# The closing normalisations and the W1 slices of an expert layer: which engine does them

## The reference

```python
x = x + _layernorm(_L0_attn_ref(_layernorm(x), ...))
x = x + _layernorm(_L0_ffn_ref(_layernorm(x), ...))
# inside _L0_ffn_ref:
y = _layer_norm(x + _mha(x, Wqkv, bqkv, Wo, bo), g1, be1)
idx = argmax(y @ Wg.T)                        # one of 8 experts for each token
moe = relu(y @ W1[idx] + b1[idx]) @ W2[idx] + b2[idx]
z = _layer_norm(y + moe, g2, be2)             # W1: 8 x 128 x 512, W2: 8 x 512 x 128
```

## Time and profile before

| | us |
|---|---|
| median of 3 runs | 722.99 |
| the runs | 721.63, 722.99, 728.51 |
| the profiled execution, its own time | 718.0 |
| its span, first to last instruction | 715.9 |
| PE, DVE, ACT, POOL busy in the span | 575.5, 428.6, 348.5, 333.9 |
| mean granted clock of TensorE | 0.891 |

### The profile page before, as it was taken

How to read it: one execution, slowest core, us unless ns; L and a number is a source line. 1 busy time by engine, 2 the same in 40 slices (tenths; PEclk the granted TensorE clock), 3 DMA queues, 4 the chain that set the end, 5 groups by cost and what they waited for, 6 DMA issues and landing times. The chain is left out here.

```text
span 715.9 us, 16711 instructions
## 1 busy us (share of the span) xinstructions
PE 575.5 (80%) x5511; PEld 428.5 (60%) x5511; DVE 428.6 (60%) x1212; ACT 348.5 (49%) x927; POOL 333.9 (47%) x579
## 2 busy tenths in 40 slices
PE   4899999999999999999834898888874059999400
PEld 3566666666666666666523787777753059998400
DVE  2454576766666666666313787878974316778630
ACT  1024566556656656655621798878640002343330
POOL 5312123332333322321236247777778601689886
PEclk9558999999999999999975999999996569999855
DMA  5000000000000000000025000000011245677223
GB/s 151 10 2 2 3 3 16 18 17 16 8 12 18 17 17 18 17 16 18 17 45 155 1 1 3 1 1 0 8 36 42 82 127 153 161 180 179 32 26 29
DMA packets 33168, 29.73 MB, mean 42 GB/s; under 512 B 4121, under 2 KB 27457, under 8 KB 33090
## 3 DMA queue, kind: packets, MB, share of 16 engines
q1 hardware_dynamic: 25906, 23.55, 12.7%
q0 software_dynamic: 6640, 4.92, 4.6%
q10 hardware_dynamic: 544, 0.26, 0.1%
HBM read 18.24 MB, written 8.12 MB: 37 GB/s over the span
## 5 line engine op out<-in xcount | busy, mean ns | idle before, releaser
L383 DVE TENSOR_REDUCE nmax<-psA 128x2 f32<-128x512 f32 x256 | 165.1, 688 | 120.7 <-PE psA L206 120.5
L511 ACT ACTIVATE pr<-psB 128x512 f32<-128x512 f32 x250 | 135.8, 595 | 123.8 <-PE psB L223 123.1
L206 PE MATMUL psA<-km,q 24*128 24x256 f32 x768 | 138.9, 425 | 3.8 <-POOL km L603 2.1
L223 PE MATMUL psB<-q,km 26*128 26x256 f32 (+1 forms) x752 | 109.9, 411 | 0.0
L206 PEld LDWEIGHTS psA<-km,q 24*128 24x128 f32 x768 | 91.3, 196 | 29.4 <-issue 17.5
L603 POOL TENSOR_TENSOR km<-kraw,rows_of 128x768 f32<-128x768 f32 x16 | 23.5, 1466 | 118.1 <-DVEq L362 113.9
L237 PE MATMUL psO<-pr,v 128*32 128x256 f32 x1024 | 69.4, 389 | 1.3 <-ACT osb L505 1.1
L223 PEld LDWEIGHTS psB<-q,km 26*128 26x128 f32 (+1 forms) x752 | 69.0, 189 | 0.2 <-issue 0.2
L1587 POOL DMA_INDIRECT out<-wz,ys x39 | 63.1, 1618 | 9.2 <-issue 7.4
L577 POOL TENSOR_SCALAR ve<-mv_r 128x2 f32<-128x2 f32 x16 | 3.7, 231 | 123.6 <-DVE mv_r L344 123.6
L1473 DVE TENSOR_TENSOR hT<-psH,e_nb1T 128x512 f32<-128x512 f32 x39 | 27.0, 692 | 42.5 <-PE psH L1434 31.1
(11 more groups left out here) (202 smaller groups left out, 1214.6 us busy)
## 6 DMA issues: line engine op xcount, KB each, us to landing
own<-W SPq DMA_DIRECT2D x39, 256.0 KB, 2.7
ys<-y_sorted SPq DMA_DIRECT2D x39, 72.0 KB, 2.2
xs<-x_all SPq DMA_DIRECT2D x16, 128.0 KB
out<-x_all SPq DMA_DIRECT2D x16, 128.0 KB, 3.7
e_w<-W SPq DMA_DIRECT2D x4, 512.0 KB
x_all<-x SPq DMA_DIRECT2D x1, 1536.0 KB, 10.1
q<-mT SPq DMA_DIRECT2D x64, 4.0 KB
out<-wz,ys POOLq DMA_INDIRECT x39, 3.4
```

What stands on the lines that cost most here:

```text
L206: last = T.matmul(psA[:, n % 2, c * L1:(c + 1) * L1], queries(b, h, depth, slice(c * P, (c + 1) * P)), keys(b, h, depth, slice(0, L1)), st ...
L223: last = T.matmul(bank_of(b, h)[:, c * L1:(c + 1) * L1], keys(b, h, depth, slice(c * P, (c + 1) * P)), queries(b, h, depth, slice(0, L1)), ...
L383: V.tensor_reduce(nmax[:, b % 2, :, h], psA[:, n % 2, :].rearrange("p (c m) -> p c m", c=2), AX.X, ALU.max, negate=True).then_inc(S["a_fre ...
L511: A.activation(pr[:, h % PRING, :, :].rearrange("p c l -> p (c l)"), bank_of(b, h), ACT.Exp, scale=SCALE1).then_inc(S["b_free"], 1)
```

## The change

In its core:

```diff
-            V.tensor_scalar(w1_i[:, :], owner[:, :], float(P), None, ALU.mult).then_inc(S["owner_ok"], 1)
+            V.tensor_scalar(w1_i[:, :], owner[:, :], float(DF), None, ALU.mult).then_inc(S["owner_ok"], 1)
...
-    t = {"w2": [P, NF, NE * P], "b1n": [NE * NF, P], "b2r": [1, NE * P], "g2r": [P, P],
+    t = {"w1": [P, NE * DF], "w2": [P, NF, NE * P], "b1n": [NE * NF, P], "b2r": [1, NE * P], "g2r": [P, P],
          "be2r": [P, P], "nb1T": [P, NE * NF], "b1T": [P, NE * NF], "b2p": [P, NE * P], "top": [P, P]}
     t = {name: ctx.enter_context(nc.sbuf_tensor("e_" + name, shape, F32)) for name, shape in t.items()}
-    loads = [(t["w2"][:, f, :].rearrange("p (e d) -> p e d", d=P),
+    loads = [(t["w1"][:, :].rearrange("p (e f) -> p e f", f=DF), W1.rearrange("e d f -> d e f"))]
+    loads += [(t["w2"][:, f, :].rearrange("p (e d) -> p e d", d=P),
...
-        own = sb("own", [P, 4, DF])
+        own = sb("own", [P, 3, DF])
...
-                pe.wait_ge(S[f"own{t % 4}"], 16 * (t // 4 + 1))
+                pe.wait_ge(S["own_ok"], t + 1)
...
-                dve.wait_ge(S[f"agg{kind}"], g)
+                dve.wait_ge(S[f"rs{kind}"], g)
                 for k in range(SIZES[g]):
                     last = V.bn_aggr(mv[kind][:, k, :], st[kind][:, k, :])
                 last.then_inc(S[f"mv{kind}"], 1)
-                dve.wait_ge(S[f"mv{kind}"], g + 1)
+
+            def scales(kind, g):
+                n, s = SIZES[g], g % 2
+                dve.wait_ge(S[f"sd{kind}"], g + 1)
                 if g >= 2:
-                    dve.wait_ge(S[f"rs{kind}"], g - 1)
-                n = SIZES[g]
-                V.tensor_scalar(nm[kind][:, g % 2, 0:n], mv[kind][:, 0:n, 0], -1.0, None, ALU.mult)
-                V.tensor_scalar(ve[kind][:, g % 2, 0:n], mv[kind][:, 0:n, 1], EPS, None, ALU.add
-                                ).then_inc(S[f"agg{kind}"], 1)
+                    dve.wait_ge(S["w_ok" if kind else "z1_ok"], ends(g - 2))
+                V.reciprocal(rs[kind][:, s, 0:n], sd[kind][:, 0:n]).then_inc(S[f"inv{kind}"], 1)
+                dve.wait_ge(S[f"inv{kind}"], g + 1)
+                V.scalar_tensor_tensor(out=nb[kind][:, s, 0:n], in0=mv[kind][:, 0:n, 0], scalar=-1.0,
+                                       in1=rs[kind][:, s, 0:n], op0=ALU.mult, op1=ALU.mult
+                                       ).then_inc(S[f"rs{kind}"], 1)
...
+                if (g := at(t, 4)) is not None:
+                    scales(0, g)
+                if (g := at(t, 10)) is not None:
+                    scales(1, g)
...
+            def fetch(t):
+                e = act.value_load(w1_i[0:1, t:t + 1], min_val=0, max_val=(NE - 1) * DF)
+                if t >= 3:
+                    act.wait_ge(S["h_full"], t - 2)
+                A.activation(own[:, t % 3, :], w["w1"][:, bass.ds(e, DF)], ACT.Copy).then_inc(S["own_ok"], 1)
...
+            def deviation(kind, g):
+                n = SIZES[g]
+                act.wait_ge(S["consts"], 1)
+                act.wait_ge(S[f"mv{kind}"], g + 1)
+                act.wait_ge(S[f"inv{kind}"], g)
+                A.activation(sd[kind][:, 0:n], mv[kind][:, 0:n, 1], ACT.Sqrt, bias=eps[:, :]
+                             ).then_inc(S[f"sd{kind}"], 1)
...
+            fetch(0)
             turned(0)
+            fetch(1)
             turned(1)
             for t in range(STEPS):
                 if t + 2 < NS:
+                    fetch(t + 2)
                     turned(t + 2)
...
+                if (g := at(t, 3)) is not None:
+                    deviation(0, g)
+                if (g := at(t, 9)) is not None:
+                    deviation(1, g)
...
-            def scale(kind, g):
-                n, s = SIZES[g], g % 2
-                pool.wait_ge(S[f"agg{kind}"], g + 1)
-                if g >= 2:
-                    pool.wait_ge(S["w_ok" if kind else "z1_ok"], ends(g - 2))
-                G.tensor_tensor(rs[kind][:, s, 0:n], ve[kind][:, s, 0:n], half4[:, 0:n], ALU.pow
-                                ).then_inc(S[f"pow{kind}"], 1)
-                pool.wait_ge(S[f"pow{kind}"], g + 1)
-                G.tensor_tensor(nb[kind][:, s, 0:n], nm[kind][:, s, 0:n], rs[kind][:, s, 0:n], ALU.mult
-                                ).then_inc(S[f"rs{kind}"], 1)
...
-                if (g := at(t, 3)) is not None:
-                    scale(0, g)
-                if (g := at(t, 9)) is not None:
-                    scale(1, g)
...
-            rows = W1.rearrange("e d f -> (e d) f")
-
-            def fetch(t):
-                e = sp.value_load(w1_i[0:1, t:t + 1], min_val=0, max_val=(NE - 1) * P)
-                if t >= 4:
-                    sp.wait_ge(S["h_full"], t - 3)
-                sp.dma_start(own[:, t % 4, :], rows[bass.ds(e, P), :]).then_inc(S[f"own{t % 4}"], 16)
-
-            def load(t):
+            sp.wait_ge(sent, 16 * NT)
+            for t in range(NS):
                 r = sp.value_load(row_i[0:1, t:t + 1], min_val=0, max_val=LAST_ROW - P)
                 if t >= RING:
...
-            for t in range(4):
-                fetch(t)
-            sp.wait_ge(sent, 16 * NT)
-            for t in range(6):
-                load(t)
-            for t in range(NS):
-                if t + 6 < NS:
-                    load(t + 6)
-                if t + 4 < NS:
-                    fetch(t + 4)
```

More of the change, by code:

```diff
@@ L1359, in expert_weights, with experts @@
     return t, loads
-def experts(nc, w, W1, ident, kept, sorting, sent, y_sorted, out):
+def experts(nc, w, ident, kept, sorting, sent, y_sorted, out):
     with ExitStack() as ctx:
@@ L1381, in experts @@
         mv = [sb(f"mv_z{k}", [P, 4, 2]) for k in range(2)]
-        nm = [sb(f"nm_z{k}", [P, 2, 4]) for k in range(2)]
-        ve = [sb(f"ve_z{k}", [P, 2, 4]) for k in range(2)]
+        sd = [sb(f"sd_z{k}", [P, 4]) for k in range(2)]
         rs = [sb(f"rs_z{k}", [P, 2, 4]) for k in range(2)]
         nb = [sb(f"nb_z{k}", [P, 2, 4]) for k in range(2)]
-        half4 = sb("half4", [P, 4])
+        eps = sb("eps", [P, 1])
         psT, psH, psO = pb("psT"), pb("psH"), pb("psO")
-        names = ["consts", "t_full", "yT_ok", "h_full", "h_ok", "o_full", "z0_ok", "st0", "st1", "mv0",
-                 "mv1", "agg0", "agg1", "pow0", "pow1", "rs0", "rs1", "z1_ok", "z2_step", "z2_ok", "w_ok"]
-        names += [f"own{r}" for r in range(4)] + [f"ys{r}" for r in range(RING)] + [f"put{r}" for r in range(WRING)]
+        names = ["consts", "t_full", "yT_ok", "own_ok", "h_full", "h_ok", "o_full", "z0_ok", "st0", "st1", "mv0",
+                 "mv1", "sd0", "sd1", "inv0", "inv1", "rs0", "rs1", "z1_ok", "z2_step", "z2_ok", "w_ok"]
+        names += [f"ys{r}" for r in range(RING)] + [f"put{r}" for r in range(WRING)]
         S = {n: ctx.enter_context(nc.semaphore("ex_" + n)) for n in names}
@@ L1433, in hidden @@
                 for f in range(NF):
-                    last = T.matmul(psH[t % 2][:, f * P:(f + 1) * P], own[:, t % 4, f * P:(f + 1) * P],
+                    last = T.matmul(psH[t % 2][:, f * P:(f + 1) * P], own[:, t % 3, f * P:(f + 1) * P],
                                     yT[:, t % 3, :], start=True, stop=True)
@@ L1570, in _ @@
             G = nc.gpsimd
-            G.memset(half4[:, :], -0.5).then_inc(S["consts"], 1)
-            pool.wait_ge(S["consts"], 1)
-            def scale(kind, g):
-                n, s = SIZES[g], g % 2
-                pool.wait_ge(S[f"agg{kind}"], g + 1)
-                if g >= 2:
-                    pool.wait_ge(S["w_ok" if kind else "z1_ok"], ends(g - 2))
-                G.tensor_tensor(rs[kind][:, s, 0:n], ve[kind][:, s, 0:n], half4[:, 0:n], ALU.pow
-                                ).then_inc(S[f"pow{kind}"], 1)
-                pool.wait_ge(S[f"pow{kind}"], g + 1)
-                G.tensor_tensor(nb[kind][:, s, 0:n], nm[kind][:, s, 0:n], rs[kind][:, s, 0:n], ALU.mult
-                                ).then_inc(S[f"rs{kind}"], 1)
+            G.memset(eps[:, :], EPS).then_inc(S["consts"], 1)
             def put(t):
@@ L1658, in build_program @@
                          minus_half, xs, y_all, logits, w, loaded, loads, y_sorted, slots, slot_i, base, sorting, sent)
-        experts(nc, w, a["W1"], ident, kept, sorting, sent, y_sorted, out)
+        experts(nc, w, ident, kept, sorting, sent, y_sorted, out)
 def kernel(L0_attn_x, L0_attn_w_qkv, L0_attn_b_qkv, L0_attn_w_o, L0_attn_b_o, L0_ffn_Wqkv, L0_ffn_bqkv, L0_ffn_Wo,
```

## The result

The changed kernel took 702.16 us (median; 701.39 to 709.53, 4 runs), beside 725.75 us for the kernel before in the same runs: a ratio of 0.970 (95% interval 0.9625 to 0.9775). Two later measurements of both kernels gave 0.977 (0.9707 to 0.9834) and 0.970 (0.9648 to 0.9757), with medians of 708.33 and 703.22 against 724.0 and 723.6. By the three pairs of medians the saving is 16 to 24 us. The forecast was 706 us, with 16.5 us saved.

The account below looks back on a forecast made before the run. VectorE was taken to bound the stream from tile 11, POOL's put queue the end. Span 715.9 - 3.3 - 13.2 = 699.4, saving 16.5 us; from the 722.99 median that gives 706 us, range 697 to 715.

Parts of the forecast that it names:

- Start: Start of the experts' stage: without W1 fetches the first `ys` load issues 4.9 us earlier, worth 4.6 after a table load.
- The copy: ScalarE's W1 fetch per tile: 0.48 us plus 0.4 register load, hidden with 0.37 us of room per tile.
- Table load: ScalarE's change to Sqrt: one load suffices, charged 0.3 us, bounds 0 and 1.3.
- The rival with loads in pairs: ScalarE: table loads around every square root, 35 us over the forecast, 741 us; chance 0.05.
- Stream: Tiles 11 to 38, paced by VectorE: 9.69 us per four tiles, tile 38's `hT` at 667.6, 3.3 us earlier.
- rival B: VectorE's cycle is shorter, 9.1 us per four tiles: 702 us, or 698 at PE's pace throughout; chance 0.14.
- Tail: Tile 38's `hT` to the last put's end: 28.2 us against 41.4 before, 13.2 saved.
- Rival D: GpSimd's puts do not draw together, still one each 2.6 us at the end: 8 us lost, 714; chance 0.04.
- recorded signs of being wrong: Profile after: VectorE waits for `sd_z`, ScalarE shows no idle time, or table loads come in pairs.
- The median: Whole kernel: the 16.5 us saving taken from the timed runs' median, 722.99, gives 706.5, called 706.

Follow-up runs that it names:

- the deviations alone: Only the deviations moved (square root on ScalarE, reciprocal and product on VectorE), W1's slices by DMA as in the kernel before: 711.06 us, 0.980 of before.

## Why the prediction was right

The direction, the range (697 to 715) and the mechanism held: the powers left GpSimd, its closing queue shrank from 41 us to 28, and VectorE set the pace from tile 11 on. Not all terms were right, and the sum owes something to luck. Point by point.

*Start.* Forecast 4.6 us saved, measured 10.8 to 6.1, 4.7. The assumption that the sends had landed holds. But 0.6 to 1.1 us are given back between tile 0 and tile 11 (23.0 and 23.3 before, 23.9 to 24.1 after), a cost that the forecast had at nothing. With the slices by DMA this part was 23.2. ScalarE's copies do not stand in PE's way there: in the timeline of the start PE waits only for `ys` (0.71 us before the second transposition) and then has no gap. What differs is its clock. It stays at half speed for 6.9 us after the first transposition, 6.7 and 6.8 in the other two profiles of this kernel, against 4.0 and 4.6 in the kernel before and 4.9 with the deviations alone, whose eight products with W2 take 1.06 us at the place where the changed kernel's take 1.61. Why the clock rises later was not tried.

*The copy.* 0.63 us alone, and 0.52 with others behind it, against 0.48 with bounds of 0.48 to 0.60, with 0.35 us for the register load where 0.4 was taken. Free, and by more than forecast, as the doubled copy shows.

*Table load.* One, 1.28 us, in front of the first square root; that one came 0.40 us late for VectorE. The `hT` of the steps around it are 2.09 to 2.15 apart, so it cost nothing where 0.3 was charged. The rival with loads in pairs fell. By the Trainium skill (ScalarE: Activation LUTs, What ACT_TABLE_LOAD costs) a drain should add 1.38 us; here the engine was idle for 1.30 before the load and ran the square root 0.02 after it, so no run shows that cost on the path.

*Stream.* This is the term that was mis-sized. The forecast was 66.3 us from tile 11 to 38, 1.3 more than before; measured were 63.0, 2.0 less. Two of its parts were off. A `scales` was taken at 0.43, a dependent pair at 0.21 each; the rows show 0.29, since only the product waits for the reciprocal, and the next instruction follows the product after 0.08. And the gap in front of `hT` behind the aggregates fell from about 0.57 to 0.43 with the two small instructions between gone, which I had held constant in the middle of the forecast and let fall in rival B. Per four tiles: 2 x 0.29 more, and the two steps with moments 0.41 and 0.45 less, a net of -0.3 where +0.3 was forecast. The sum also mixed two bases: 9.69 is 0.30 over the one cycle of 9.39 in the earlier trace rows, while the mean of six before was 9.51; on the mean the same working gives 58.9 us from tile 11 to 35 and not 58.1, further from the 55.3 measured. The pace is rival B's 9.1 per four tiles, though its gap of 0.32 is not reached.

*Tail.* Forecast 28.2, measured 28.3 to 28.5. Put 28 starts 8.14 us after tile 38's `hT` (forecast 7.6 + 0.55), and the puts draw together, 1.88 apart. Rival D fell. That 8.14 meets the forecast so closely is luck: `wz` of tile 28 is there 7.05 us after that `hT`, 1.1 earlier than the working had it (each of three `scales` is 0.14 cheaper, and the last two aggregates stand behind the scales and not before, among smaller differences). The puts of tiles 26 and 27 are still in front, although the forecast said that POOL is not behind then. The small queue took up what VectorE was early. Of the recorded signs of being wrong, one showed in part: VectorE does wait for `sd_z`, 2.6 us in all, though not in the steady stream. The square root was expected to be late once, by 0.5 (0.41 in the row), and was so five times in the tail; behind the puts' queue this cost nothing that shows.

*The median.* In the stage 19 us were won where 16.5 were forecast. The kernel before had medians of 723.6 to 725.75 in all later measurements, and the profile that I had was 5.6 to 7.8 us below that, of which the pad writes explain 5. I had set the saving against the median and not against that profile (701.5 would have come out), which this confirms: the hold is in both kernels and drops out of the difference. What is left of the distance between 706 and 702 is the stream's 3 us and the spread of the two stages before, whose end (DVE's last index) lies between 561.0 and 569.3 us in the fourteen profiles of this study, with the 2 MB transfer and without it.

## What to carry to other kernels

Follow the wait chain to the engine that closes the kernel, but then size the stream behind it by the distance of starts on its busiest in-order engine: here VectorE, whose register load of 0.3 to 0.4 us in front of each `hT`, movable in a few lines, gave 5.2 us in the stage, more than the whole resident copy of W1 (3.7 to 4.4). An operation that waits for another engine's small result can go on an engine with room as long as its in-order neighbours leave a step in between; the square root had one in the stream, and cost nothing there. A term that comes out to the hundredth can still hide two errors: look at what the instruction itself waited for, not only at when it started. One profile of an execution can be several us from the median for a cause outside the change; when the two disagree, set the saving, not the end, against the median.

## What the runs showed of the hardware that I had not expected

A direct DMA issued while GpSimd issues indirect ones can take its engine far longer than 1.1 us: eight writes took 16.2 to 16.5 us on SyncE (ten profiles), 15.3 on ScalarE, and four took 3.8 us once the sends had landed. It is not an even 2 us a write. In the changed kernel's third profile the eight start at 558.98, 562.4, 566.6 and 570.9 and then 1.0 to 1.1 apart, while the last send is issued at 568.1. The instructions of the pad line, of the changed kernel's second profile and then of the kernel before's first one (durations in ns, min/median/max):

```profile
L1335 SPq MOVE y_sorted<-zeros x8: 13/29/704, 562.1 to 578.0; - x8
```

```profile
L1335 SPq MOVE y_sorted<-zeros x8: 29/29/43, 559.0 to 566.9; - x8
```

A register move that takes 29 ns takes up to 704 during the hold. The first profile of the kernel before had the same overlap and no hold. What decides between the two is open and was not tried. Small instructions on VectorE (128x4) cost 0.21 us to one that waits for their result and 0.08 to one that does not. And where one queue issued two transfers for each tile, 1.1 us apiece, TensorE waited 2.5 us for `ys` between its first three tiles and ran at 0.56 of full speed in the second 8 us of the stage, against 0.93 with one transfer for each tile.
